# Causal attention layer: the masks of query tiles 0 and 1 added to the scores on TensorE, their maxima taken over several heads in one plain operation each

## The chip, the cores and the metric

The kernel runs on one core of a Trainium2 chip. The metric is the device time of one launch in microseconds. Three runs of the kernel before took 2162.98, 2170.28 and 2160.96 us, with a median of 2162.98. The engines are named TensorE (PE in the profile, its weight loads PEld), VectorE (DVE), ScalarE (ACT), GpSimd (POOL) and SyncE (SP).

## The reference

Nine layers are applied in turn to x of 8 sequences x 512 tokens x 128 features, each with a layer norm ahead and a residual behind. The change lies in the first, causal attention with 16 heads of 8 features:

```
q = x @ Wq.T + bq ; k, v alike; each split in 16 heads of 8
dot = einsum('bhqd,bhkd->bhqk', q, k)
dot = where(tril(ones(t, t)), dot, -inf) / sqrt(128)
out = softmax(dot) @ v, heads put side by side, @ Wo.T + bo
```

Behind it come a modulus layer, a second attention layer (not causal, with rotary positions), the modulus again, linear attention, a GELU network, a layer in simulated FP4, attention with the softmax over queries, and FP4 again.

## The kernel before

Layers run one after the other, and all engines meet between them. In the attention layer each of the 8 sequences is an item, its 16 heads are done in four head groups of four heads, and its 512 tokens are four tiles of 128.

q and k are split into three bf16 parts and stacked on 72 rows, so that one bf16 product of depth 96 gives a score at nearly float32 precision. The stacks are QS and KS. A head group goes through two phases.

The first phase finds each query's largest score. `first_scores` (L466 and behind, the matmul is L477) computes scores with queries on the partitions, one unit at a time into one of two PSUM banks. `score_units` lists the units of a causal head group: query tile 0 is one unit with all four heads (128 keys each), tile 1 is two units with two heads each (256 keys), and tiles 2 and 3 are one unit for each head (384 and 512 keys). That is 11 units in a head group. `maxima` (L601 and behind) takes a unit's maxima on VectorE. In the causal layer it does so for each head with a custom operation (L609) that adds a row of mask values to the scores, writes the sum as bf16 to a scratch tile and keeps the maximum. A small second instruction (DVE_READ_ACCUMULATOR2) then writes the maximum out. In the layer that is not causal it is one plain reduction for a unit (L614). `max_ready` counts the units that TensorE has finished and `max_free` those that VectorE has read. TensorE waits at each unit until the one two before it has been read.

`negate` (L621, L623) then makes the negated maxima of the group, TensorE turns them (L485), ScalarE copies them (L389), and a DMA puts them as two more rows into QS.

The second phase runs two groups later. `scores` (L501) computes the scores with keys on the partitions and the maxima already taken off, ScalarE takes the exponential (L414), GpSimd sets the future part of each diagonal tile to zero (L315), TensorE sums the values (L519), and the sums are turned (L433) and divided on VectorE (L628, L630). Once in a sequence come the layer norm (L558 to L574 on VectorE), the projections of q, k and v (L454, L458, L463; copied out by ScalarE in L369, L375 and L382), their split on GpSimd (L256 to L262), and the output projection (L536).

The order of all this is a list of events with due times, `attention_order`, sorted once. Each engine walks this one list and does its own part of each event, in that order, so the phases of different groups are interleaved alike on all engines. The transpose of the maxima, the projections and the turned sums share one PSUM bank, `misc`, in turn. Constants are made once by GpSimd: `ident16` is the identity in bf16, and `mask_qk` a 128 x 128 bf16 tile with zeros where the key is not behind the query and -1e30 elsewhere. It is made in the kernel before too, but not used in this layer.

Of the kernel before, what the change touches and what calls it, by code (L numbers as in the profile page):

```python
# [25 lines left out]
P = 128  # L26
# [56 lines left out]
SHIFT_ROWS = 2  # L83
SHIFT_AT = 96
LAG = 2


def score_units(causal):
# [12 lines left out]
def attention_order(items, causal):  # L101
# [4 lines left out]
    def at(time, what, n, q, i=0):  # L106
        found.append((time, len(found), what, n, q, i))
# [12 lines left out]
    for n in range(items):  # L120
# [22 lines left out]
        for q in range(QUADS):  # L143
# [6 lines left out]
            for i, t in enumerate(s_at):  # L150
                at(g + LAG + t, "scores", n, q, i)
            for i, t in enumerate(sum_at):
                at(g + LAG + t, "sum", n, q, i)
            at(g + LAG + copy_at, "copy", n, q)
            at(g + LAG + (1.50 if causal else 1.44), "tail", n, q)
        at(QUADS * n + 3 + LAG + 1.62, "oT", n, 0)
        at(QUADS * n + 3 + LAG + 1.82, "y", n, 0)
    return [event[2:] for event in sorted(found)]


def attention(core, items, w, causal, rope, scale):
    nc, X, ps = core["nc"], core["X"], core["ps"]
# [39 lines left out]
    FIRST, SECOND, SUMS, MISC = 0, 2, 6, 7  # L202
# [227 lines left out]
    def tensor(pe):  # L430
# [35 lines left out]
        def first_scores(n, q, gq, u):  # L466

            qt, heads, width, stride = first[u]
            U = N1 * gq + u
            if q % 2 == 0 and u == 0:  # L470

                pe.wait_ge(stack_loaded[q // 2], 16 * STACK_DMAS * (n + 1))
            if U >= 2:
                pe.wait_ge(max_free, U - 1)
            for o, j in enumerate(heads):
                h = 4 * q + j
                last = pe.matmul(ps[:, FIRST + U % 2, o * stride:o * stride + width],  # L477
                                 QS[n % 2][0:SHIFT_AT, h, qt * P:(qt + 1) * P], KS[n % 2][0:SHIFT_AT, h, 0:width],
                                 start=True, stop=True)
            last.then_inc(max_ready, 1)  # L480

        def turn_nm(n, q, gq, i):
# [50 lines left out]
        def out(n, q, gq, i):  # L533
            own_misc("y", n)
            for t in range(4):
                last = pe.matmul(misc4[:, t, :], oT[:, t, :], w["wo"][:], start=True, stop=True)  # L536
            last.then_inc(misc_full, 1)

        walk({"bias": fold_bias, "xT": new_xT, "q": project_q, "k": project_k, "v": values,
              "first": first_scores, "nm": turn_nm, "scores": scores, "sum": sum_keys,  # L540
              "tail": tail, "oT": turn_O, "y": out})

    def vector(v):
# [54 lines left out]
        def maxima(n, q, gq, u):  # L598
            qt, heads, width, stride = first[u]
            U = N1 * gq + u  # L600
            src = ps[:, FIRST + U % 2, :].rearrange("p (h c) -> p h c", c=stride)[:, 0:len(heads), 0:width]  # L601
            v.wait_ge(max_ready, U + 1)
            if u == 0 and gq > 1:
                v.wait_ge(nm_ready, gq - 1)
            if causal:
                if U >= 4:
                    v.wait_ge(max_free, U - 3)
                for o, j in enumerate(heads):
                    last = v.tensor_tensor_reduce(masked[U % 4][:, o * stride:o * stride + width], src[:, o, :], mask_row[:, 512 - width:512],  # L609
                                                  1.0, 4 * NEG, ALU.add, ALU.max,  # L610
                                                  accum_out=M[gq % 2][:, j, qt:qt + 1])
                last.then_inc(max_free, 1)
            else:
                v.tensor_reduce(M[gq % 2][:, heads[0]:heads[-1] + 1, qt], src, AX.X, ALU.max).then_inc(max_free, 1)  # L614
# [18 lines left out]
        def residual(n, q, gq, i):  # L633
# [5 lines left out]
        walk({"clear": clear_stacks,  # L639
              "bias": total_bias, "stat": stat, "spread": spread, "norm": norm, "turn": prepare, "split": split_part,  # L640
              "first": maxima, "negate": negate, "tail": tail, "y": residual})

    return dict(gpsimd=gpsimd, sync=sync, scalar=scalar, tensor=tensor, vector=vector)
# [1275 lines left out]
```

## Time and profile before

| | us | share |
|---|---|---|
| profiled execution | 2163.62 | |
| its span, first to last instruction | 2161.9 | |
| TensorE matmuls busy | 1738.2 | 80% |
| TensorE weight loads busy | 962.5 | 45% |
| VectorE busy | 1507.8 | 70% |
| ScalarE busy | 959.2 | 44% |
| GpSimd busy | 654.6 | 30% |
| the masked maxima of this layer (L609), 512 operations | 227.3 | |

The causal layer runs up to about 400 us of the span. Its first scores and maxima run from 42 to 379 us. Matmuls are pipelined: the record of a single one holds its travel through the array too, so consecutive records overlap, and the distance between starts says what one costs in a row. The same holds for VectorE, where an operation may start before the record of the one ahead has ended. The timeline merges like instructions that follow each other: "x4" with a length is the length of all four together.

### The profile page before, as it was taken

The page shows a single profiled execution, that of the slowest core. Times are in us where ns is not written, and L with a number is a line of the kernel's source. Part 1 is how long each engine was busy: PE and PEld are TensorE (multiplying, and loading weights), DVE is VectorE, ACT ScalarE, POOL GpSimd, SP SyncE. Part 2 cuts the span into 40 slices and gives each one's busy share as a digit, 9 for nine tenths or more (in the row PEclk, how much of TensorE's full clock was granted, in tenths as well). Part 3 has the DMA queues.
Part 4 walks back from the last instruction along what each step waited for, and adds up shares of the span by engine and source line. Part 5 has one row for each costly group of instructions (what it writes and reads, how often), then busy time and mean ns, then how long its engine had stood idle before and what let it go on. Part 6 is the DMA issues. An engine that isn't in the chain of part 4 may idle for free. (4 is left out here: it accounts for less than half of the span.)

```text
span 2161.9 us, 37483 instructions
## 1 busy us (share of the span) xinstructions
PE 1738.2 (80%) x12706; PEld 962.5 (45%) x12781; DVE 1507.8 (70%) x4131; ACT 959.2 (44%) x1598; POOL 654.6 (30%) x658
## 2 busy tenths in 40 slices
PE   3789999647999999985799999999978466687666
PEld 1344334322333333323466666666656244455444
DVE  4788888446888888836556666566654899556997
ACT  1466666423666666664444444444433122232122
POOL 5454563342222222004000000000013666301666
PEclk9899999757999999996999999999999688798887
DMA  6443232014221222000000000000000000000000
GB/s 113 113 62 70 46 57 35 1 15 73 45 46 43 37 43 41 19 1 1 1 1 2 2 2 2 3 1 2 2 1 0 1 0 0 1 1 1 5 15 20
DMA packets 56689, 49.80 MB, mean 23 GB/s; under 512 B 9220, under 2 KB 54468, under 8 KB 56516
## 3 DMA queue, kind: packets, MB, share of 16 engines
q1 hardware_dynamic: 51748, 44.67, 10.6%
q10 hardware_dynamic: 4768, 2.89, 0.9%
q8 instruction: 100, 1.64, 0.3%
q14 instruction: 73, 0.60, 0.1%
HBM read 7.10 MB, written 2.10 MB: 4 GB/s over the span
## 5 line engine op out<-in xcount | busy, mean ns | idle before, releaser
L614 DVE TENSOR_REDUCE ab_M<-ps 128x1 f32<-128x512 f32 x512 | 332.6, 686 | 90.3 <-PE ps L477 88.7
L477 PE MATMUL ps<-KS,QS 96*128 96x512 bf16 (+3 forms) x1024 | 325.1, 353 | 74.3 <-DMA KS<-aa_splitk 20.1
L414 ACT ACTIVATE ab_probs<-ps 128x1024 f32<-128x1024 f32 x256 | 260.3, 1022 | 134.9 <-PE ps L501 128.3
L609 DVE CUSTOM_DVE_ANT_0 aa_masked<-ps,aa_mask_row 128x384 bf16<-128x384 f32 (+3 forms) x512 | 227.3, 487 | 73.9 <-PE ps L477 71.1
L501 PE MATMUL ps<-QS,KS 128*128 128x512 bf16 x949 | 239.0, 338 | 18.2 <-DMA KS<-signs 9.4
L477 PEld LDWEIGHTS ps<-KS,QS 96*128 96x128 bf16 x1024 | 91.0, 98 | 359.7 <-DVE ab_M L614 160.8
L414 ACT ACTIVATE aa_probs<-ps 128x1024 f32<-128x1024 f32 (+1 forms) x192 | 166.6, 881 | 126.1 <-PE ps L501 125.6
L1572 PE MATMUL ps<-gate_up,fp_xT 128*128 128x352 f32 x256 | 128.4, 667 | 93.0 <-DVE fp_xh L1614 91.5
L675 POOL TENSOR_TENSOR la_rstd<-la_vare,mhalf 128x4 f32<-128x4 f32 x16 | 16.1, 1008 | 442.4 <-DVE la_vare L670 442.4
L519 PE MATMUL ps<-ab_probs,ab_V 128*9 128x512 f32 x1024 | 133.9, 594 | 14.3 <-ACT ab_C L421 9.9
L315 POOL TENSOR_SCALAR_AFFINE_SELECT aa_probs<-aa_probs 128x256 f32<-128x256 f32 (+1 forms) x192 | 93.0, 486 | 166.9 <-ACT aa_probs L414 166.1
L1195 DVE SCALAR_TENSOR_TENSOR la_phiq<-ps,la_ezq 128x512 f32<-128x512 f32 x64 | 44.2, 690 | 126.0 <-ACT la_ezq L1053 126.0
L1572 PEld LDWEIGHTS ps<-gate_up,fp_xT 128*128 128x128 f32 x256 | 68.3, 280 | 139.8 <-issue 67.8
L501 PEld LDWEIGHTS ps<-QS,KS 128*128 128x128 bf16 x1024 | 91.4, 98 | 83.9 <-issue 28.5
L1529 ACT ACTIVATE fp_silu<-ps 128x352 f32<-128x352 f32 x64 | 29.7, 465 | 190.5 <-PE ps L1572 190.5
L1140 PE MATMUL ps<-la_V,la_S 128*64 128x65 f32 x2048 | 103.0, 221 | 0.0
L1044 ACT ACTIVATE la_V<-ps 128x512 f32<-128x512 f32 x64 | 38.2, 597 | 138.8 <-PE ps L1086 138.8
L519 PE MATMUL ps<-aa_probs,aa_V 128*9 128x512 f32 (+3 forms) x1024 | 92.9, 435 | 4.4 <-POOL aa_probs L315 3.5
L1051 ACT ACTIVATE la_belowq<-ps 128x512 f32<-128x512 f32 x64 | 38.2, 597 | 130.1 <-PE ps L1093 130.1
L1140 PEld LDWEIGHTS ps<-la_V,la_S 128*64 128x64 f32 x2048 | 91.6, 137 | 0.2 <-issue 0.2
L1204 DVE TENSOR_TENSOR la_S<-ps,keep_kq 128x512 f32<-128x512 f32 x128 | 82.4, 685 | 4.9 <-PE ps L1112 1.9
L1136 PE MATMUL ps<-la_state,la_phiq 128*64 128x130 f32 x768 | 75.5, 275 | 0.0
(302 smaller groups left out, 3603.1 us busy)
## 6 DMA issues: line engine op xcount, KB each, us to landing
QS<-aa_splitq SPq DMA_DIRECT2D x144, 64.0 KB
QS<-ab_splitq SPq DMA_DIRECT2D x144, 64.0 KB
KS<-aa_splitk SPq DMA_DIRECT2D x126, 64.0 KB
KS<-ab_splitk SPq DMA_DIRECT2D x126, 64.0 KB
out<-X SPq DMA_DIRECT2D x8, 256.0 KB, 2.3
KS<-aa_splitk ACTq DMA_DIRECT2D x18, 64.0 KB
KS<-ab_splitk ACTq DMA_DIRECT2D x18, 64.0 KB
w_raw<-fp_weights SPq DMA_DIRECT2D x1, 560.0 KB, 5.1
```

The source lines that it names most:

```text
L315: g.affine_select(out=diagonal, in_=diagonal, compare_op=ALU.is_ge, fill=0.0, base=0, pattern=[[0, len(heads)], [1, P]], channel_multiplie ...
L414: act.activation(v(probs[u % 4][:]), v(src), ACT.Exp, scale=scale).then_inc(scores_free, 1)
L477: last = pe.matmul(ps[:, FIRST + U % 2, o * stride:o * stride + width], QS[n % 2][0:SHIFT_AT, h, qt * P:(qt + 1) * P], KS[n % 2][0:SHIFT_A ...
L501: last = pe.matmul(ps[:, bank, c:c + width], KS[n % 2][:, h, kt * P:(kt + 1) * P], QS[n % 2][:, h, 512 - width:512], start=True, stop=True)
L519: last = pe.matmul(ps[32 * j:32 * j + DH + 1, SUMS, 512 - width:512], V[n % 2][:, kt, 4 * q + j, :], probs[(N2 * gq + u) % 4][:, o * strid ...
L609: last = v.tensor_tensor_reduce(masked[U % 4][:, o * stride:o * stride + width], src[:, o, :], mask_row[:, 512 - width:512], 1.0, 4 * NEG, ...
L614: v.tensor_reduce(M[gq % 2][:, heads[0]:heads[-1] + 1, qt], src, AX.X, ALU.max).then_inc(max_free, 1)
L1136: pe.matmul(outs[rows, c, 0:2 * AUG], phi[0][j % 4][:, c * P:(c + 1) * P][:, rows], state[j % 2][:, c - 1, :], start=True, stop=False)
L1140: last = pe.matmul(outs[rows, c, AUG * a:AUG * (a + 1)], S[a][j % 2][:, c * P:(c + 1) * P][:, rows], V[par][:, c, 2 * j + a, :], start=c = ...
L1195: v.scalar_tensor_tensor(phi[a][j % (4 - 2 * a)][:], ps[:, PHI + a, :], 0.0, ez[a][:], ALU.max, ALU.add)\
L1204: v.tensor_tensor(S[a][j % 2][:].rearrange("p (c q) -> p c q", c=4), ps[:, SCORES + a, :].rearrange("p (c q) -> p c q", c=4), over(core["k ...
L1572: last = pe.matmul(ps[:, GATE_UP + 2 * t + i, 0:INNER], xT[p][:, t * P:(t + 1) * P], gate_up[:, i, :], start=True, stop=True)
```

## The change

For query tiles 0 and 1 of the causal layer (`ADDED_MASKS = 2`) each matmul of the first scores is left open, and a second one with `ident16` as its weights adds `mask_qk` to the last 128 columns of that head's scores, the diagonal tile. The masked scores then stand in PSUM, and `maxima` takes the path of the other layer: one plain reduction for a unit, with four results for tile 0 and two for each half of tile 1. Tiles 2 and 3 stay as they were.

```diff
--- before.py
+++ after.py
@@ -83,6 +83,7 @@
 SHIFT_ROWS = 2
 SHIFT_AT = 96
 LAG = 2
+ADDED_MASKS = 2
 
 
 def score_units(causal):
@@ -474,9 +475,14 @@
                 pe.wait_ge(max_free, U - 1)
             for o, j in enumerate(heads):
                 h = 4 * q + j
+                adds = causal and qt < ADDED_MASKS
                 last = pe.matmul(ps[:, FIRST + U % 2, o * stride:o * stride + width],
                                  QS[n % 2][0:SHIFT_AT, h, qt * P:(qt + 1) * P], KS[n % 2][0:SHIFT_AT, h, 0:width],
-                                 start=True, stop=True)
+                                 start=True, stop=not adds)
+                if adds:
+                    end = o * stride + width
+                    last = pe.matmul(ps[:, FIRST + U % 2, end - P:end], core["ident16"][:], core["mask_qk"][:],
+                                     start=False, stop=True)
             last.then_inc(max_ready, 1)
 
         def turn_nm(n, q, gq, i):
@@ -602,7 +608,7 @@
             v.wait_ge(max_ready, U + 1)
             if u == 0 and gq > 1:
                 v.wait_ge(nm_ready, gq - 1)
-            if causal:
+            if causal and qt >= ADDED_MASKS:
                 if U >= 4:
                     v.wait_ge(max_free, U - 3)
                 for o, j in enumerate(heads):
```

On TensorE, the place where the first scores of query tiles 0 and 1 stand, between tile 3 of the same head group and the transpose of the maxima. Before:

```order
L477 MATMUL ps<-KS,QS 128x128 [waits aa_max_free,aa_stack_loaded0]
L477 MATMUL ps<-KS,QS 128x128 x3
L519 MATMUL ps<-aa_probs,aa_V 9x256 [waits aa_probs_masked]
L519 MATMUL ps<-aa_probs,aa_V 9x256 x3
L501 MATMUL ps<-QS,KS 128x512 [waits aa_scores_free,aa_nm_loaded2]
L501 MATMUL ps<-QS,KS 128x512
L477 MATMUL ps<-KS,QS 128x256 [waits aa_max_free]
L477 MATMUL ps<-KS,QS 128x256
```

The same place in the changed program (line numbers are those of the changed file; L479 is the score matmul, L484 the mask matmul, L507 the second phase's scores, L525 the value sums):

```order
L479 MATMUL ps<-KS,QS 128x128 [waits aa_max_free,aa_stack_loaded0]
L484 MATMUL ps<-mask_qk,ident 128x128
L479 MATMUL ps<-KS,QS 128x128
L484 MATMUL ps<-mask_qk,ident 128x128
L479 MATMUL ps<-KS,QS 128x128
L484 MATMUL ps<-mask_qk,ident 128x128
L479 MATMUL ps<-KS,QS 128x128
L484 MATMUL ps<-mask_qk,ident 128x128
L525 MATMUL ps<-aa_probs,aa_V 9x256 [waits aa_probs_masked]
L525 MATMUL ps<-aa_probs,aa_V 9x256 x3
L507 MATMUL ps<-QS,KS 128x512 [waits aa_scores_free,aa_nm_loaded2]
L507 MATMUL ps<-QS,KS 128x512
```

Eight matmuls have come in for each head group, one behind each matmul of tiles 0 and 1, and nothing has changed places.

On VectorE, from the maxima of tile 0 to the second half of tile 1, with the negation of the group before between them. Before (ISA is the masked operation, the row with 128x1 its accumulator reading):

```order
L609 ISA aa_masked,aa_M<-ps,aa_mask_row 128x128 [waits aa_max_free,aa_nm_ready,aa_max_ready]
L609 ISA aa_M 128x1
L609 ISA aa_masked,aa_M<-ps,aa_mask_row 128x128
L609 ISA aa_M 128x1
L609 ISA aa_masked,aa_M<-ps,aa_mask_row 128x128
L609 ISA aa_M 128x1
L609 ISA aa_masked,aa_M<-ps,aa_mask_row 128x128
L609 ISA aa_M 128x1
L621 TENSOR_SCALAR aa_nm<-aa_M 128x16 [waits aa_misc_full,aa_max_free]
L623 TENSOR_TENSOR aa_nm<-aa_M,aa_nm 128x16
L609 ISA aa_masked,aa_M<-ps,aa_mask_row 128x256 [waits aa_max_free,aa_max_ready]
L609 ISA aa_M 128x1
```

In the changed program (L620 is the plain reduction, L615 the masked operation of tile 2, L627 and L629 the negation):

```order
L620 TENSOR_REDUCE aa_M<-ps 128x4 [waits aa_nm_ready,aa_max_ready]
L627 TENSOR_SCALAR aa_nm<-aa_M 128x16 [waits aa_misc_full,aa_max_free]
L629 TENSOR_TENSOR aa_nm<-aa_M,aa_nm 128x16
L620 TENSOR_REDUCE aa_M<-ps 128x2 [waits aa_max_ready] x2
L615 ISA aa_masked,aa_M<-ps,aa_mask_row 128x384 [waits aa_max_free,aa_max_ready]
L615 ISA aa_M 128x1
L615 ISA aa_masked,aa_M<-ps,aa_mask_row 128x384 [waits aa_max_free,aa_max_ready]
```

Sixteen rows of tiles 0 and 1, with their accumulator readings, have become three in each head group, and their waits for `max_free` have gone.

## Rows read from the trace of the kernel before

**Rows 1.** Busy time by stretch: the stretch, its length, then each engine's busy us.
```profile
60.00:100.00 40.00, 28.16 (x206) 11.97 (x211) 27.45 (x126) 18.20 (x26) 14.32 (x24) 0.84 0.41 107
...
200.00:250.00 50.00, 46.25 (x375) 21.65 (x379) 41.10 (x185) 30.84 (x43) 25.64 (x39) 1.00 0.37 62
```

**Rows 2.** Waits, 60 to 480 us: total us, how many, longest.
```profile
PEld ps L477 <- DVE aa_M L609: 60.2, 118, 1.6
DVE aa_masked L609 <- PE ps L477: 52.0, 91, 7.7
```

**Rows 3.** Groups by line, VectorE, 60 to 440 us: busy us, mean ns | idle.
```profile
L609 DVE CUSTOM_DVE_ANT_0 aa_masked<-ps,aa_mask_row 128x256 bf16<-128x256 f32 x120 | 44.7, 421 | 13.0 <-PE ps L477 12.2
L609 DVE DVE_READ_ACCUMULATOR2_ANT aa_M<- 128x1 f32 x480 | 39.7, 83 | 0.0
L609 DVE CUSTOM_DVE_ANT_0 aa_masked<-ps,aa_mask_row 128x128 bf16<-128x128 f32 x120 | 27.5, 286 | 0.2 <-PE ps L477 0.2
```

**Rows 4.** Timeline, VectorE, group with the layer norm: start us, length us.
```profile
300.05 0.28 DVE L609 CUSTOM_DVE_ANT_0 aa_masked<-ps,aa_mask_row 128x128 bf16<-128x128 f32 x1
...
300.88 0.17 DVE L621 TENSOR_SCALAR aa_nm<-aa_M 128x16 bf16<-128x16 f32 x1
...
301.82 0.42 DVE L609 CUSTOM_DVE_ANT_0 aa_masked<-ps,aa_mask_row 128x256 bf16<-128x256 f32 x1
...
302.51 0.42 DVE L609 CUSTOM_DVE_ANT_0 aa_masked<-ps,aa_mask_row 128x256 bf16<-128x256 f32 x1
...
303.31 0.34 DVE L574 TENSOR_SCALAR aa_xn<-X,aa_meanvar,aa_rstd 128x128 f32<-128x128 f32 x1
303.57 0.55 DVE L609 CUSTOM_DVE_ANT_0 aa_masked<-ps,aa_mask_row 128x384 bf16<-128x384 f32 x1
```

**Rows 5.** Reductions elsewhere: groups by line, then timelines of VectorE and TensorE.
```profile
L614 DVE TENSOR_REDUCE ab_M<-ps 128x1 f32<-128x512 f32 x512 | 332.6, 686 | 90.3 <-PE ps L477 88.7
...
L1404 DVE TENSOR_REDUCE fp_xh0amax<-fp_xh 128x60 f32<-128x960 f32 x14 | 16.1, 1153 | 1.3
...
641.68 2.54 DVE L614 TENSOR_REDUCE ab_M<-ps 128x1 f32<-128x512 f32 x4 [0.67 <-PE ps L477]
...
641.91 0.90 PE L477 MATMUL ps<-KS,QS 96*128 96x512 bf16 x2
```

**Rows 6.** Groups by line, TensorE, 60 to 440 us, then 1500 to 2162.
```profile
L501 PE MATMUL ps<-QS,KS 128*128 128x128 bf16 x128 | 12.4, 219 | 0.0
...
L903 PE MATMUL ps<-w_w,mlp_up 128*128 128x128 f32 x256 | 29.7, 275 | 0.0
```

**Rows 7.** Timelines, 276 to 283 us: TensorE, then GpSimd.
```profile
277.52 0.39 PE L501 MATMUL ps<-QS,KS 128*128 128x128 bf16 x4
...
278.57 0.38 PE L477 MATMUL ps<-KS,QS 96*128 96x128 bf16 x4 [0.44 <-DVE aa_M L609]
...
280.80 0.41 PE L519 MATMUL ps<-aa_probs,aa_V 128*9 128x128 f32 x8 [0.34 <-POOL aa_probs L315]
...
280.10 0.64 POOL L315 TENSOR_SCALAR_AFFINE_SELECT aa_probs<-aa_probs 128x512 f32<-128x512 f32 x1
```

**Rows 8.** Timeline, TensorE at 262 us, then ScalarE at 291 us.
```profile
262.16 0.34 PE L477 MATMUL ps<-KS,QS 96*128 96x384 bf16 x1 [0.50 <-DVE aa_M L609]
...
291.59 0.60 ACT L382 ACTIVATE aa_V<-ps 128x512 f32<-128x512 f32 x1
```

**Rows 9.** Timeline, TensorE, 289 to 305 us.
```profile
290.50 1.05 PE L463 MATMUL ps<-w_wv,aa_xT 128*128 128x128 f32 x8
...
291.82 0.39 PE L477 MATMUL ps<-KS,QS 96*128 96x256 bf16 x2
292.33 0.22 PE L485 MATMUL ps<-ident,aa_nm 128*32 128x128 bf16 x1
...
302.65 0.34 PE L477 MATMUL ps<-KS,QS 96*128 96x384 bf16 x1 [0.33 <-DVE aa_M L609]
...
304.19 0.34 PE L477 MATMUL ps<-KS,QS 96*128 96x384 bf16 x1 [0.51 <-DVE aa_M L609]
```

## The prediction

> **What bounds the kernel now.** I read the page's slices first, then the busy time by stretch, then who waited for whom, then the timeline of one whole sequence, engine by engine. In the stretch from 200 to 250 us TensorE is busy 46.25 of 50 us and VectorE 41.10 [rows 1], so neither of them has the stage to itself, and the busy time of TensorE contains waits, because a record of 128 columns lasts 219 ns though four of them take only 0.39 us [rows 6, 7]. The waits go both ways: TensorE's weight loads for the first scores waited 60.2 us for VectorE's maxima, and the maxima waited 52.0 us for the first scores [rows 2]. The two engines hand two PSUM banks to and fro in a fixed order, and each unit waits for whichever is late. One sequence takes 42.03 us, read from the third matmul of query tile 2 to the same matmul of the next sequence (262.16 and 304.19) [rows 8, 9]. It holds four head groups. There are 32 groups in all, and the first two lie in the startup, where transfers decide. So 30 groups count, or 7.5 sequences.
>
> **VectorE's part.** The records of one group's query tiles 0 and 1 are 4 x 0.286 + 4 x 0.421 + 8 x 0.083 = 3.49 us [rows 3], and three reductions of 512 elements would be 3 x 0.686 = 2.06 us [rows 5]. That difference, 1.43 us, is not what is saved, since records overlap. From the start of the first 128-wide operation to the negation are 0.83 us for four (300.05 to 300.88), and from the first 256-wide one at 301.82 to the third at 302.51 are 0.69 us for two [rows 4]. Four reductions in a row take 2.54 us, which is (2.54 - 0.69) / 3 = 0.62 us from one to the next [rows 5]. So tile 0 goes from 0.83 to 0.62 us and tile 1 from 1.38 to 1.24 us: 0.35 us a group. The strided reduction with four results is not in the trace. The nearest row is the one with 60 results of 16 elements each: 960 elements take 1.153 us, against 0.686 for 512 with one result [rows 5], so 448 elements more cost 0.47 us, 1.04 ns each, and the 59 further results nothing that shows. I take 0.62 us; the other end is four separate operations, as slow as now (0.83), a gain of nothing. A little more comes from the handover: the first matmul of tile 2 starts 0.83 us after the first 256-wide operation (302.65 against 301.82) [rows 4, 9], while in the other layer the next matmul may start 0.75 us after its reduction starts (641.68; the second of two matmuls at 641.91, lasting to 642.81 together, starts near 642.43) [rows 5].
>
> **TensorE's part.** Each group gets eight matmuls of 128 columns with their own weight load. Price: four pairs of load and matmul with 128 columns take 0.39 us, the last of them 0.219, so (0.39 - 0.219) / 3 = 0.057 us from one to the next [rows 6, 7]. 8 x 0.057 = 0.46 us a group. The trace has no bf16 matmul that adds to what the matmul right before it wrote. Nearest below: the accumulating float32 products of 128 columns (line 903) have the 275 ns record of any float32 matmul of that width and no idle time before them [rows 6], so I take no stall. The other end is a mask matmul that waits until the product under it has landed, a full 0.219 us each. The lower end is zero, where all eight fall into waits.
>
> The Trainium skill ("TensorE: Matmul & The Clock Gate", section "Back-to-back issue gap") speaks against the change here: it says that a stream of load and matmul pairs with 128 columns sustains about 81 ns each, and only an isolated pair about 56 ns. By 81 ns the eight would be 0.65 us a group. The trace's 57 ns is for such pairs too, but only for runs of four; the new run of tile 0 is eight long.
>
> **What of it lies on the path.** I follow one sequence from 262.16 and carry the shift along, a mask being 0.057 us.
> - The group in which q and k are projected: the four masks of tile 0 and the two of the first half of tile 1 stand in an unbroken run of TensorE. The last two hide, since the transpose of the maxima waits for ScalarE to copy q out of the same PSUM bank. +0.34.
> - The group at 278.57: tile 0 waits 0.44 for VectorE there, but that VectorE operation itself waited for TensorE, so the shift stays, and four masks are added behind it. Six masks (0.34 us) then run into the 0.34 us in which the value sums at 280.80 wait for GpSimd's masking, which started at 280.10 and lasts 0.64 [rows 7]. Two masks behind it remain. +0.11.
> - The group with the value projection: six masks on an unbroken run. The values (290.50) are copied by ScalarE at 291.59 for 0.60 us, and the transpose at 292.33 waits for that. The second half of tile 1, at 291.82, takes 2 x 0.107 + 2 x 0.057 at most until 292.15 with its masks, so the last two hide [rows 8, 9]. +0.34.
> - The group with the layer norm (300.05 to 304.19): here VectorE is the bound. The matmuls at 302.65 and 304.19 wait 0.33 and 0.51 us for it [rows 9], and its chain from 300.05 to 303.57 has no wait on TensorE in it. It becomes shorter by 0.83 - 0.62 = 0.21 for tile 0, by 0.14 for tile 1, and the drain and accumulator reading before the normalisation at 303.31 (0.11 behind the last operation) go: 0.46 in all. TensorE comes later by the sum so far, 0.79, and by this group's eight masks, 0.46, which is 1.25. It had some 0.50 us to spare at 302.65 (two 512-column matmuls before it), and the scores of that matmul then lay another 0.5 us before VectorE took them up at 303.57. What is over, 0.25, is below the 0.79 - 0.46 at which VectorE arrives. So VectorE still decides. -0.46.
>
> Sum: 0.34 + 0.11 + 0.34 - 0.46 = +0.33 us a sequence, x 7.5 = +2.5 us. Between 60 and 100 us the granted clock is 0.84 on average [rows 1]; the masks of one or two groups cost double there, +0.3. Together +2.8 us. The profiled execution took 2163.62 us (span 2161.9 and 1.7 around it), so its counterpart should take 2166.4. The median of the three runs shown, 2162.98, is 0.6 lower, so the predicted median is 2165.8. Nothing behind 380 us changes; it only shifts. The wait for the bank counter four units back that goes with the masked operations costs nothing now, since VectorE itself raised it.
>
> **Rivals.** With 0.5% I mean 10.8 us, about what a measurement of this kernel can tell from no change.
> - VectorE decides everywhere. For it: the 60.2 us of waits behind the maxima. Then each group gains what the layer norm group gains, 30 x 0.46 = 14 us: 2149. Against it: in three groups of four the VectorE operation that TensorE waits for had itself waited for TensorE's scores. Chance 8%. That even the recorded 1.43 us go (32 x 1.43 = 46, 2117) gets 2%.
> - The mask matmul waits for the product that it adds to (slower). It would take place at each of the eight masks, at 0.219 us instead of 0.057. 32 x 0.219 = 7.0 us a sequence, less some 1.6 us of waits that swallow a part, is 5.4, x 7.5 = 40 us: 2203. It decides from about 0.10 us a mask, where the total passes 10.8 us. Softer form: the weight loads, whose records last 98 ns, show in a run of eight; 0.098 a mask gives 0.59 + 0.48 + 0.59 - 0.3 = 1.4 us a sequence, 2174. For it: no such run in the trace. Against it: runs of four at 57 ns, in which a load of 98 ns would show already. Chance 14% for both.
> - The reduction gains nothing, so that only TensorE's part remains: 0.79 and in the layer norm group 0.1 to 0.4, some 1.1 us a sequence, 2171. It is still within 0.5% and is counted there.
>
> By the skill's 81 ns, an estimate from its page, the same walk gives 0.49 + 0.34 + 0.49 - 0.46, or 0.9 us a sequence, and 2170; that too would be no change that can be told.
>
> **Chances and range.** The forecast, no measurable change, gets 76% (with the third rival inside it), faster 10%, slower 14%. The forecast's own range is 2159 to 2172. Between the faster and slower rivals I cut at a little more on each side: 2157 to 2175.
>
> **What would show it.** In the changed profile the reductions of query tiles 0 and 1 should read about 0.69 us, 96 of them, and the maxima's busy time should fall by some 40 us with hardly any gain in time. VectorE's idle time before the remaining masked operations should grow. In the run of eight, starts should be 0.057 us apart: tile 0's eight in 0.62 us with the last one's tail. One sequence should take 42.4 us. I am wrong if a sequence takes under 41 or over 43.5 us, if the run of eight takes over 0.9 us, or if TensorE still waits 60 us for the maxima.

## The result, and the profile after

The changed kernel took 2174.4 us (median of 15 runs, 2165.87 to 2178.32) against 2163.44 us (15 runs, 2160.93 to 2172.84). The ratio is 1.0042 with a 95% interval of 1.0028 to 1.0056, which is 9 us slower (the medians themselves lie 11 us apart). The interval lies clear of 1, so the kernel did become slower, but by less than the 0.5% up to which the prediction spoke of no change. The forecast was +2.8 us with a range of 2157 to 2175. The median lies 0.6 us under the upper end of that range, so the question is where the other 6 us came from. The profiled execution took 2170.27 us, its span was 2168.6.

Totals of a whole kernel are a blunt measure here. From the last negation of the causal layer to the end, which is the same code in all variants, the profiled executions took between 1775 and 1784 us. The causal layer repeats itself much more exactly: most sequences of one kernel agree within 0.04 us. Now and then one is longer, up to 1.3 us in one profile, and in nearly all of these TensorE waited once for the transfer of the maxima into QS (1.08 us at 132 us of the kernel before). So below I give the length of a typical sequence beside each ratio. It is the distance between negations that lie four head groups apart. Before: 42.02 us. After: 43.17 (from 43.16 to 43.19 in four of six, 43.79 in one and 43.08 in the last).

The busy time of the stretch from 200 to 250 us after the change; columns as in [rows 1]:

```profile
200.00:250.00 50.00, 46.25 (x387) 22.48 (x391) 38.72 (x120) 30.85 (x43) 28.71 (x42) 1.00 0.34 59
```

TensorE still reads 46.25 us, VectorE 38.72 instead of 41.10. The last three figures are the granted clock, the busy share of the DMA engines and GB/s. The waits between 60 and 480 us, the answer to [rows 2] (L479 is the score matmul, L615 the masked operation, L620 the reduction, L484 the mask matmul):

```profile
PEld ps L479 <- DVE aa_M L615: 53.0, 92, 1.4
DVE aa_masked L615 <- PE ps L479: 42.8, 91, 0.9
...
DVE aa_M L620 <- PE ps L484: 25.1, 34, 8.1
```

The wait of TensorE's weight loads for the maxima fell from 60.2 to 53.0 us and VectorE's waits for scores rose from 52.0 to 67.9. The groups of maxima over the whole span, busy us and mean ns, answering to [rows 3]:

```profile
L615 DVE CUSTOM_DVE_ANT_0 aa_masked<-ps,aa_mask_row 128x384 bf16<-128x384 f32 (+1 forms) x256 | 152.0, 621 | 44.8 <-PE ps L479 44.0
...
L620 DVE TENSOR_REDUCE aa_M<-ps 128x2 f32<-128x512 f32 (+1 forms) x96 | 65.8, 690 | 46.8 <-PE ps L484 45.0
...
L615 DVE DVE_READ_ACCUMULATOR2_ANT aa_M<- 128x1 f32 x256 | 21.2, 83 | 0.0
```

The masked operations, their accumulator readings and the reductions are 152.0 + 21.2 + 65.8 = 239.0 us. The masked maxima alone were 227.3 us before, and with 512 readings of 0.083 us they were 269.7. So 30.7 us of recorded time went and none of it came back as time.

TensorE's timeline, one layer norm group's run of tile 0 and then the points that mark the groups: the third matmul of tile 2 (269.00) and the transposes of the maxima (277.94, 288.82, 300.10):

```profile
263.86 0.22 PE L479 MATMUL ps<-KS,QS 96*128 96x128 bf16 x1 [0.44 <-DVE aa_M L615]
263.91 0.22 PE L484 MATMUL ps<-mask_qk,ident 128*128 128x128 bf16 x1
263.97 0.22 PE L479 MATMUL ps<-KS,QS 96*128 96x128 bf16 x1
...
264.26 0.22 PE L484 MATMUL ps<-mask_qk,ident 128*128 128x128 bf16 x1
...
269.00 0.34 PE L479 MATMUL ps<-KS,QS 96*128 96x384 bf16 x1 [0.96 <-DVE aa_M L615]
...
277.94 0.23 PE L491 MATMUL ps<-ident,aa_nm 128*32 128x128 bf16 x1
...
288.82 0.23 PE L491 MATMUL ps<-ident,aa_nm 128*32 128x128 bf16 x1
...
300.10 0.22 PE L491 MATMUL ps<-ident,aa_nm 128*32 128x128 bf16 x1
```

The next sequence's layer norm group, its transpose and its third matmul of tile 2:

```profile
309.81 0.23 PE L491 MATMUL ps<-ident,aa_nm 128*32 128x128 bf16 x1
...
312.20 0.34 PE L479 MATMUL ps<-KS,QS 96*128 96x384 bf16 x1 [0.97 <-DVE aa_M L615]
```

The same marks in the kernel before are 262.16 [rows 8], 292.33 and 304.19 [rows 9], and these three, from its TensorE timeline:

```profile
270.70 0.22 PE L485 MATMUL ps<-ident,aa_nm 128*32 128x128 bf16 x1
```

```profile
281.46 0.23 PE L485 MATMUL ps<-ident,aa_nm 128*32 128x128 bf16 x1
```

```profile
301.56 0.23 PE L485 MATMUL ps<-ident,aa_nm 128*32 128x128 bf16 x1
```

In the run of eight the starts lie 0.057 us apart (263.86 to 264.26 for seven steps; 0.058 in most runs of eight of this profile and 0.060 in the others). Take 262.16 and 269.00 as the common zero. The shift at each mark is then the predicted walk measured:

| at | before | after | shift measured | shift predicted |
|---|---|---|---|---|
| transpose, group with q and k | 270.70 | 277.94 | +0.40 | +0.34 |
| transpose, group at 278 us | 281.46 | 288.82 | +0.52 | +0.45 |
| transpose, group with v | 292.33 | 300.10 | +0.93 | +0.79 |
| transpose, group with the layer norm | 301.56 | 309.81 | +1.41 | +1.25 |
| third matmul of tile 2, group with the layer norm | 304.19 | 312.20 | +1.17 | +0.33 |

Three groups went as predicted, with 0.06 and 0.07 us more in the first and the third. At the fourth transpose TensorE is late by all eight masks of that group too, again about as predicted. The error lies behind it: the last step was to give back 0.46 and cost another 0.24. The timeline of VectorE in that group shows the new wait:

```profile
264.64 0.68 DVE L620 TENSOR_REDUCE aa_M<-ps 128x4 f32<-128x512 f32 x1
...
266.01 0.17 DVE L571 TENSOR_SCALAR aa_vare<-aa_meanvar 128x4 f32<-128x4 f32 x1
266.09 1.33 DVE L620 TENSOR_REDUCE aa_M<-ps 128x2 f32<-128x512 f32 x2
268.12 0.35 DVE L580 TENSOR_SCALAR aa_xn<-X,aa_meanvar,aa_rstd 128x128 f32<-128x128 f32 x1 [0.70 <-POOL aa_rstd L283]
268.38 0.55 DVE L615 CUSTOM_DVE_ANT_0 aa_masked<-ps,aa_mask_row 128x384 bf16<-128x384 f32 x1
```

VectorE was done with both halves of tile 1 at about 267.4 and then stood idle for 0.70 us until 268.12. GpSimd, from the same stretch:

```profile
266.70 0.41 POOL L316 TENSOR_SCALAR_AFFINE_SELECT aa_probs<-aa_probs 128x256 f32<-128x256 f32 x1 [2.16 <-ACT aa_probs L415]
267.07 1.02 POOL L283 TENSOR_TENSOR aa_rstd<-aa_vare,mhalf 128x4 f32<-128x4 f32 x1
```

and GpSimd in the kernel before, with VectorE's normalisation at 303.31 [rows 4]:

```profile
301.88 0.41 POOL L315 TENSOR_SCALAR_AFFINE_SELECT aa_probs<-aa_probs 128x256 f32<-128x256 f32 x1 [1.92 <-ACT aa_probs L414]
302.25 1.02 POOL L282 TENSOR_TENSOR aa_rstd<-aa_vare,mhalf 128x4 f32<-128x4 f32 x1
```

The normalisation needs the root of the variance, which GpSimd computes in 1.02 us. It ended at 303.27 before and at 268.09 now, each time 0.03 to 0.04 us ahead of the normalisation. The variance itself was ready long before (266.18). GpSimd is late because the masking of the first probabilities stands ahead of the root in its order. That masking waits for ScalarE's exponential, which waits for the scores on TensorE, and those stand behind tile 0's eight matmuls. The scores and the exponential, after and before:

```profile
265.19 0.38 PE L507 MATMUL ps<-QS,KS 128*128 128x512 bf16 x1 [0.16 <-issue]
...
265.61 1.02 ACT L415 ACTIVATE aa_probs<-ps 128x1024 f32<-128x1024 f32 x1 [1.77 <-PE ps L507]
```

```profile
300.37 0.38 PE L501 MATMUL ps<-QS,KS 128*128 128x512 bf16 x1 [0.16 <-issue]
...
300.78 1.02 ACT L414 ACTIVATE aa_probs<-ps 128x1024 f32<-128x1024 f32 x1 [1.53 <-PE ps L501]
```

The exponential waits 1.77 us for the scores instead of 1.53. These 0.24 us are the four masks of tile 0, and GpSimd's wait for the exponential grew by the same (2.16 against 1.92). So in this group too the chain runs over TensorE, and VectorE's gain went into a wait.

### The profile page after: what moved, and what is told of

It is laid out like the page before. It is cut to its first block and busy times, and to the rows that moved or that the text cites. A ratio compares the mean times of both kernels' runs of the same rounds, so it can differ in the third digit from the quotient of the medians.

```text
span 2168.6 us, 37516 instructions
## 1 busy us (share of the span) xinstructions
PE 1753.8 (81%) x12962; PEld 982.4 (45%) x13037; DVE 1492.6 (69%) x3715; ACT 960.0 (44%) x1598; POOL 654.9 (30%) x658
## 5 line engine op out<-in xcount | busy, mean ns | idle before, releaser
L479 PE MATMUL ps<-KS,QS 96*128 96x512 bf16 (+3 forms) x1024 | 335.7, 353 | 74.6 <-DMA KS<-aa_splitk 20.6
L620 DVE TENSOR_REDUCE ab_M<-ps 128x1 f32<-128x512 f32 x512 | 332.7, 686 | 90.6 <-PE ps L479 89.1
L479 PEld LDWEIGHTS ps<-KS,QS 96*128 96x128 bf16 x1024 | 97.7, 98 | 351.1 <-DVE ab_M L620 160.2
L507 PE MATMUL ps<-QS,KS 128*128 128x512 bf16 x949 | 239.0, 338 | 18.0 <-DMA KS<-signs 9.5
L615 DVE CUSTOM_DVE_ANT_0 aa_masked<-ps,aa_mask_row 128x384 bf16<-128x384 f32 (+1 forms) x256 | 152.0, 621 | 44.8 <-PE ps L479 44.0
L525 PE MATMUL ps<-ab_probs,ab_V 128*9 128x512 f32 x1024 | 133.9, 594 | 14.4 <-ACT ab_C L422 9.8
L507 PEld LDWEIGHTS ps<-QS,KS 128*128 128x128 bf16 x1024 | 91.5, 98 | 84.3 <-issue 28.3
L620 DVE TENSOR_REDUCE aa_M<-ps 128x2 f32<-128x512 f32 (+1 forms) x96 | 65.8, 690 | 46.8 <-PE ps L484 45.0
L525 PE MATMUL ps<-aa_probs,aa_V 128*9 128x512 f32 (+3 forms) x1024 | 92.9, 435 | 2.6 <-POOL aa_probs L316 2.5
```

The source lines that it names most:

```text
L507: last = pe.matmul(ps[:, bank, c:c + width], KS[n % 2][:, h, kt * P:(kt + 1) * P], QS[n % 2][:, h, 512 - width:512], start=True, stop=True)
L525: last = pe.matmul(ps[32 * j:32 * j + DH + 1, SUMS, 512 - width:512], V[n % 2][:, kt, 4 * q + j, :], probs[(N2 * gq + u) % 4][:, o * strid ...
```

## The experiments

Each ran beside the kernel before, which had a median of 2164.8 us beside the first four and of 2163.9 us beside the last three.

**TensorE's half alone.** The mask matmuls as in the change, the maxima as before:

```diff
-            if causal and qt >= ADDED_MASKS:
+            if causal:
```

> TensorE's half alone: the eight mask matmuls of a head group are there, and query tiles 0 and 1 still take their maxima with the masked operation, which adds the mask row a second time. Theory T (after the result): nothing of VectorE's shorter part reaches the end, because the chain runs over TensorE in three groups of a sequence and in the layer norm group over TensorE's scores, ScalarE's exponential, GpSimd's masking and its root of the variance. Then this kernel costs what the full change costs: a sequence of 43.0 to 43.3 us (before 42.02, changed 43.19) and 8 to 11 us over the kernel before. Rival R: the 0.35 to 0.46 us of VectorE do count in the layer norm group, and the masks are dearer than thought. Then this kernel is 3 us or more above the full change: 12 to 14 us over the kernel before, a sequence of 43.6.

Measured: ratio 1.0060 (1.0038 to 1.0081), a sequence of 43.94 us. The sequence is longer than either theory said, and the time, 13 us over before, is the rival's. But the surplus of 0.77 us over the full change does not lie where the two differ, in the layer norm group. That group's stretch, from its negation to the next, took 10.41 us in both kernels, and its normalisation waits for GpSimd here as well, only 0.26 us in place of 0.70:

```profile
271.52 0.34 DVE L580 TENSOR_SCALAR aa_xn<-X,aa_meanvar,aa_rstd 128x128 f32<-128x128 f32 x1 [0.26 <-POOL aa_rstd L283]
```

So in the full change VectorE's shorter part is worth nothing there, which is theory T. The surplus lies in the stretch from the negation of the group that began at 278 us in the kernel before. It took 11.59 us here and 10.81 with the full change, while the other three agree within 0.02. VectorE's timeline there, the negation and the first maxima of tile 1:

```profile
290.69 0.70 DVE L627 TENSOR_SCALAR aa_nm<-aa_M 128x16 bf16<-128x16 f32 x1
291.47 1.17 DVE L629 TENSOR_TENSOR aa_nm<-aa_M,aa_nm 128x16 bf16<-128x16 f32 x1
292.56 0.41 DVE L615 CUSTOM_DVE_ANT_0 aa_masked<-ps,aa_mask_row 128x256 bf16<-128x256 f32 x1
```

and GpSimd's, its masking and a part of the split of k:

```profile
290.73 0.63 POOL L316 TENSOR_SCALAR_AFFINE_SELECT aa_probs<-aa_probs 128x512 f32<-128x512 f32 x1
291.33 1.27 POOL L261 TENSOR_TENSOR aa_splitk<-aa_restk,zeros 128x512 bf16<-128x512 f32 x1
```

TensorE's transpose, which needs their result:

```profile
292.69 0.23 PE L491 MATMUL ps<-ident,aa_nm 128*32 128x128 bf16 x1 [0.43 <-DVE aa_nm L629]
```

VectorE's two small operations are recorded with 0.70 and 1.17 us, and they end within 0.1 us of GpSimd's operations beside them. Where GpSimd is idle they take 0.17 and 0.18 us; at this place they take 0.34 and 0.51 with the full change, and 0.35 and 0.51 in the kernel before. So this kernel has a collision that the other two have in a milder form, and here it reaches TensorE.

**VectorE's half alone.** No mask matmuls, reductions for tiles 0 and 1 over unmasked scores:

```diff
-                adds = causal and qt < ADDED_MASKS
+                adds = False
```

> VectorE's half alone: plain reductions for tiles 0 and 1 over scores to which no mask was added, so these maxima are taken over later keys too; no mask matmuls. Theory T: in the layer norm group the normalisation waited only 0.11 us behind VectorE's own last maximum in the kernel before, so only about 0.1 us a sequence is gained before the root of the variance from GpSimd decides: a sequence of 41.9 us, the kernel 0 to 2 us faster than before, and VectorE idle some 0.4 us in front of the first normalisation, released by GpSimd. Rival R: the whole 0.46 us count, a sequence of 41.55 and 3.5 us faster.

Measured: 0.9986 (0.9971 to 1.0002), a sequence of 42.02 us, just as before; even the 0.1 us that the theory gave it did not come. VectorE in the layer norm group:

```profile
258.37 0.68 DVE L620 TENSOR_REDUCE aa_M<-ps 128x4 f32<-128x512 f32 x1
...
259.74 0.17 DVE L571 TENSOR_SCALAR aa_vare<-aa_meanvar 128x4 f32<-128x4 f32 x1
259.82 1.28 DVE L620 TENSOR_REDUCE aa_M<-ps 128x2 f32<-128x512 f32 x2
261.61 0.35 DVE L580 TENSOR_SCALAR aa_xn<-X,aa_meanvar,aa_rstd 128x128 f32<-128x128 f32 x1 [0.51 <-POOL aa_rstd L283]
```

The reductions are done at about 261.1 and the normalisation waits 0.51 us for GpSimd's root. The shorter chain is worth nothing by itself. The rival's 41.55 us is out.

**The full change with the root one place earlier on GpSimd.**

```diff
-        at(t0 + 0.09, "spread", n, 0)
+        at(t0 + (0.03 if causal else 0.09), "spread", n, 0)
```

> The full change, and GpSimd takes the root of the variance one place earlier, ahead of its masking of the first probabilities of that group; in the causal layer alone, and nothing else moves. Theory T: the root then follows the variance at 266.18 us at once and ends at 267.25 instead of 268.09, the first normalisation starts at about 267.45 behind the reductions instead of 268.12, so a sequence loses 0.5 to 0.7 us (42.5 to 42.7) and the kernel comes to 3 to 6 us over before. Rival R (the masks themselves on TensorE's path make the 1.17 us, the root only happens to end there): less than 1.5 us below the full change.

Measured: 1.0018 (1.0002 to 1.0034), a sequence of 42.43 to 42.46 us in three of six (the others 42.34, 42.83 and 43.03; twice in this profile TensorE waited for the transfer of the maxima, once in each of the last two). GpSimd and VectorE in the layer norm group of a typical sequence:

```profile
219.60 1.03 POOL L283 TENSOR_TENSOR aa_rstd<-aa_vare,mhalf 128x4 f32<-128x4 f32 x1 [1.73 <-DVE aa_vare L571]
```

```profile
219.34 0.17 DVE L571 TENSOR_SCALAR aa_vare<-aa_meanvar 128x4 f32<-128x4 f32 x1
219.42 1.33 DVE L620 TENSOR_REDUCE aa_M<-ps 128x2 f32<-128x512 f32 x2
220.67 0.42 DVE L580 TENSOR_SCALAR aa_xn<-X,aa_meanvar,aa_rstd 128x128 f32<-128x128 f32 x1
```

The root starts 0.09 us after the variance operation has ended (219.34 + 0.17), and the normalisation follows the reductions without a wait, 0.04 us behind the root. A sequence is 0.74 us shorter than with the change as it was, and it is 0.41 us over the kernel before, where my walk had +0.33. The whole gain lies in the layer norm group: its stretch takes 9.67 us in place of 10.41, and the other three agree with the full change within 0.01. So the root's place in GpSimd's order is what had kept VectorE's gain from counting.

**The kernel before with the same move.** The same edit on the kernel before.

> The kernel before, with the same one move of the root of the variance on GpSimd and nothing else. Theory T: the root ended 0.1 us too late there, so a sequence shortens by 0.1 us at most (41.9) and the time by 0 to 1.5 us: no change that can be told. Rival (the root was a bound before too): 3 us or more faster.

Measured: 0.9987 (0.9974 to 1.0000), a sequence of 41.92 us. The root was 0.10 us late before as well, and it was no bound worth naming until something in front of it became faster or slower. That 0.10 us also shows a misreading in the prediction: the 0.11 us ahead of the normalisation at 303.31, which it took for the masked operation's drain and accumulator reading, were this wait. With the root early the masked operations are the same and the normalisation starts together with the last accumulator reading:

```profile
302.39 0.08 DVE L609 DVE_READ_ACCUMULATOR2_ANT aa_M<- 128x1 f32 x1
302.39 0.34 DVE L574 TENSOR_SCALAR aa_xn<-X,aa_meanvar,aa_rstd 128x128 f32<-128x128 f32 x1
```

**Reductions without masks, and the root early.** The edits of the second and third experiment together, on the changed kernel.

> Plain reductions for tiles 0 and 1 without any mask added (so the maxima are taken over later keys too), no mask matmuls, and GpSimd's root of the variance one place earlier. Theory T: with the root out of the way the shorter VectorE chain of the layer norm group counts at last. Forecast 0.46 us shorter there, of which the earlier root alone gave 0.10: a sequence of 41.5 to 41.6 us (reductions alone 42.02, root alone 41.92), and about 3.5 us faster than before. Rival (VectorE's part is worth nothing anywhere): 41.9 us, as with the earlier root alone.

Measured: 0.9965 (0.9949 to 0.9981), a sequence of 41.54 us in three of six; in three others, 41.75, 41.92 and the last, TensorE waited for the transfer of the maxima. VectorE's gain is there, but only with the root out of the way: 42.02 for the reductions alone, 41.92 for the root alone, 41.54 for both. VectorE's own part of that is the 0.38 us between 41.92 and 41.54. The time fell by 7.6 us where 3.5 were expected; the profiled layer became 3.2 us shorter, and the sequences don't account for the rest. This version is faster than the kernel before by 0.35%, and by the two ratios about 0.8% faster than the full change. It subtracts maxima taken over later keys too from the scores, which cancels in the softmax as long as the exponentials of the visible keys don't underflow. That holds for the inputs here and is no promise for others.

**Each mask twice.** A second, equal mask matmul behind each:

```diff
                     last = pe.matmul(ps[:, FIRST + U % 2, end - P:end], core["ident16"][:], core["mask_qk"][:],
+                                     start=False, stop=False)
+                    last = pe.matmul(ps[:, FIRST + U % 2, end - P:end], core["ident16"][:], core["mask_qk"][:],
                                      start=False, stop=True)
```

> The full change with each mask matmul issued twice, so 16 of them in a head group. Theory T: the starts stay 0.057 us apart also in a run of twelve, and since the waits that hid some masks are nearly used up by the first eight, more than the 18 masks of a sequence that show now will show again: a sequence of 44.2 to 44.9 us against 43.17, 8 to 13 us more than the full change. Rival (each mask has waits of its own that take it): under 43.9 us. Rival (a longer run costs more for each mask): over 45.5 us.

Measured: 1.0117 (1.0090 to 1.0144), a sequence of 44.82 us, 1.65 more than with one mask each. The run of twelve on TensorE (L479 scores, L484 and L486 masks), with its last matmul:

```profile
271.69 0.22 PE L479 MATMUL ps<-KS,QS 96*128 96x128 bf16 x1 [0.44 <-DVE aa_M L617]
271.75 0.22 PE L484 MATMUL ps<-mask_qk,ident 128*128 128x128 bf16 x1
271.81 0.22 PE L486 MATMUL ps<-mask_qk,ident 128*128 128x128 bf16 x1
...
272.33 0.22 PE L486 MATMUL ps<-mask_qk,ident 128*128 128x128 bf16 x1
```

Eleven steps in 0.64 us: 0.058 us each, also where a matmul adds to what the one right before it wrote. 32 further masks at 0.058 would be 1.86 us a sequence, and 1.65 show; of the first 32 (1.86 us) 1.17 showed. In two of the four stretches all eight further masks show (0.51 and 0.52 us), so there the waits that hide masks are used up by the first eight. In the layer norm group only the four of tile 0 do (0.25), as with the full change. In the group at 278 us the collision of the first experiment is back (1.17 us, and TensorE waits 0.23 us for it), so its 0.36 us are not the masks' alone. By the ratios the time is some 16 us over the full change, more than the 8 to 13 expected, from four runs with a wide interval; the profiled layer is 12.5 us longer.

**TensorE's half alone, with GpSimd's split moved.** To the first experiment's kernel:

```diff
-                at(t0 + 1.17 + 0.44 * a + 0.11 * i, "split", n, a, i)
+                at(t0 + 1.17 + 0.44 * a + 0.11 * i + (0.25 if causal and n and a and i > 1 else 0), "split", n, a, i)
```

> The kernel with TensorE's half alone (masked operations kept), whose sequence took 43.94 us where 43.2 was expected, and in it GpSimd does the last two parts of splitting k one masking later, so that they no longer stand where VectorE makes the negated maxima. Theory C: the 0.77 us more come from VectorE's small operation at line 629, recorded at 1.17 us instead of 0.18, which is held until GpSimd's 1.27 us operation ends. With that operation moved it lasts 0.2 us again and the sequence comes down to 43.1 to 43.3 us. Rival (the 0.77 us are what VectorE's longer masked operations cost): the sequence stays at 43.9 us.

Measured: 1.0053 (1.0038 to 1.0069), a sequence of 43.68 us. VectorE at the same place, and then on TensorE the transpose, the third matmul of tile 2 and the first value sums behind it:

```profile
288.89 0.17 DVE L629 TENSOR_TENSOR aa_nm<-aa_M,aa_nm 128x16 bf16<-128x16 f32 x1
289.04 0.42 DVE L615 CUSTOM_DVE_ANT_0 aa_masked<-ps,aa_mask_row 128x256 bf16<-128x256 f32 x1
```

```profile
289.62 0.23 PE L491 MATMUL ps<-ident,aa_nm 128*32 128x128 bf16 x1
...
291.22 0.34 PE L479 MATMUL ps<-KS,QS 96*128 96x384 bf16 x1 [0.17 <-DVE aa_M L615]
...
292.74 1.05 PE L525 MATMUL ps<-aa_probs,aa_V 128*9 128x512 f32 x8 [0.43 <-POOL aa_probs L316]
```

The small operation (L629) lasts 0.17 us again and the maxima follow at once, so GpSimd's operation had held it; L627, beside a masking that was not moved, still takes 0.70. The sequence came to neither forecast: only 0.26 of the 0.77 us came back. TensorE's marks in this group tell why. Counted from the start of tile 0, the transpose stands at 3.00 us with the full change, at 3.51 with TensorE's half alone and at 3.01 here, and the third matmul of tile 2 at 4.59, 5.37 and 4.61. So up to there the whole surplus is gone with the collision, and the longer masked operations cost nothing. Behind it the value sums stand at 5.62, 6.40 and 6.14: they now wait 0.43 us for GpSimd's masking, which follows the parts of the split, and these start later than before. So the collision makes the 0.77 us, and 0.5 of them were lost again to the move that removed it.

## Why the prediction was right, and where it was off

**The outcome.** No change beyond 0.5% was forecast with 76%, and the ratio of 1.0042 is that, though the measurement can tell it from none. The sign was right and the size was not: +9 us against +2.8. That the time fell into the range is partly luck: 2174.4 lies above the forecast's own range of 2159 to 2172 and inside only what was added to it on the slower side, by 0.6 us.

**VectorE's part** was sized right but for one term. Judging by distances between starts and not by the sum of records gave 0.35 us a group instead of 1.43. The reduction with four results reads 0.687 us and the one with two 0.691, against the 0.69 foretold for all 96. The layer norm group's chain did become shorter once it was allowed to, by 0.38 us (41.54 against 41.92), where the two terms 0.21 and 0.14 give 0.35. The third term, 0.11 for drain and accumulator reading, was GpSimd's root and not VectorE's to gain. I had also said that the recorded time would fall by 40 us; it fell by 31, and VectorE's total, in which overlapping records count once, by 15 (1507.8 to 1492.6 us).

**TensorE's part** was sized right too. The price of a mask was taken as 0.057 us from four pairs in a row, and it is 0.057 to 0.060 in runs of eight and 0.058 in a run of twelve. The Trainium skill's 81 ns for such pairs ("TensorE: Matmul & The Clock Gate", "Back-to-back issue gap") did not show in any run here. That section gives its figure of about 56 ns for an isolated single matmul without its weight load, and not for an isolated pair, as the prediction has it. In the walk by 81 ns the term of the group at 278 us should be 0.31 and not 0.34, and in the one by 98 ns 0.44 and not 0.48, which changes neither total by more than 0.3 us. The rival in which a mask waits for the product under it is refuted by the same rows.

**Which masks lie on the path** was right in three of four groups (+0.93 at the third mark against +0.79), and on TensorE up to the transpose of the fourth (+1.41 against +1.25).

**The step that failed** is the last one: "So VectorE still decides. -0.46." I had checked the layer norm group's chain for waits on TensorE and found none, and overlooked that its normalisation needs a value from GpSimd. In the kernel before that value came 0.04 us ahead of the normalisation. The profile put almost no wait down to it, because two chains ended there at nearly the same time. One of them I made shorter, by some 0.4 us. The other runs over tile 0's masks, the scores, the exponential, the masking of the first probabilities and the root, and it became 0.24 us longer by tile 0's four masks. The sequence follows the later of the two. In place of -0.46 it was +0.24. With GpSimd's order changed, the stretch of the layer norm group is 9.67 us against 10.15 before, which is -0.48: about 0.10 of it is the earlier root's own and the rest VectorE's.

**The count of sequences** held: from the third group's negation to the last the layer took 308.96 us against 300.32, which is 8.6 us, or 7.25 sequences at 1.17 and a little. The startup cost more than the 0.3 us that I gave it. The third negation stands at 79.2 to 80.2 us in the four profiles without mask matmuls and at 80.0 to 81.5 in the five with them, about 1 us later in the mean. Why is open; the granted clock from 60 to 100 us was much the same, 0.84 before and 0.83 after.

**The rivals.** VectorE did not decide everywhere: its half alone moved nothing. The rival that the reduction gains nothing had the size nearest to the truth, 1.1 us a sequence and 2171 us, and for a reason akin to its own: the gain existed and did not count.

## What to carry to other kernels

When a change makes a chain shorter, look at the last operation that this chain feeds, list all that this operation needs, and read when each of them was ready. A profile that shows no wait there may only show a tie. A shift of work from an engine that waits to one that is waited for costs its full price wherever the second engine's order is unbroken, and short waits hide only the first few additions. Within a layer of repeated steps, the length of one step tells 0.1 us apart where totals of the whole kernel scatter by several.

## What the runs showed of the hardware

The two small VectorE operations of the negation, which work between SBUF tiles, are held while GpSimd works on SBUF. The 128x16 subtraction took 0.17 to 0.18 us alone, 0.51 us in the kernel before when GpSimd's masking was under way, and 1.17 us when it started behind a GpSimd operation of 1.27 us, ending with it. Not every operation is: the plain reduction and the masked operation of 512 columns, which read PSUM, took 0.68 to 0.69 us with and without GpSimd beside them, and the layer norm's statistics, which read and write SBUF, took 0.29 us both ways. A bf16 matmul of 128 columns with its own weights costs 0.057 to 0.060 us in a run of eight, also when each second one adds to the result of the one before.
